# The last short cross-attention of a perceiver kernel rebuilt: raw contexts loaded in both layouts, context statistics taken in an earlier stage

## The reference

```python
def layernorm(x, g, b):
    mu = jnp.mean(x, axis=-1, keepdims=True)
    var = jnp.mean(jnp.square(x - mu), axis=-1, keepdims=True)
    return (x - mu) * jax.lax.rsqrt(var + EPS) * g + b
x1 = layernorm(modality1, ln1_g, ln1_b)
x2 = layernorm(modality2, ln2_g, ln2_b)
q = x1 @ Wq + bq
k = x2 @ Wk + bk
v = x2 @ Wv + bv
attn = jax.nn.softmax(jnp.einsum('bqe,bke->bqk', q, k) * scaling, axis=-1)
return jnp.einsum('bqk,bke->bqe', attn, v) @ Wo + bo
```

## Time and profile before

| what | us |
|---|---|
| median of 3 runs (lowest to highest) | 2023.21 (2018.51 to 2026.66) |
| profiled execution, its own time | 2018.47 |
| its span, first to last instruction | 2016.6 |
| TensorE busy over the span | 1633.3 (81%) |
| xattn2, first load issued to the last add | 930.7 to 1279.2 |
| xattn3, first instruction to the last add | 1556.2 to 1717.0 |
| TensorE busy, granted clock in 1556.2 to 1601 | 5.80 of 44.8, 0.50 |
| TensorE busy, granted clock in 1608 to 1717 | 93.81 of 109, 0.87 |

### The profile page before, as it was taken

How to read it: one execution, slowest core, us unless ns; L and a number is a source line. 1 busy time by engine, 2 the same in 40 slices (tenths; PEclk the granted TensorE clock), 3 DMA queues, 4 the chain that set the end, 5 groups by cost and what they waited for, 6 DMA issues and landing times. The chain is left out here.

```text
span 2016.6 us, 36051 instructions
## 1 busy us (share of the span) xinstructions
PE 1633.3 (81%) x12690; PEld 1402.0 (70%) x12690; DVE 1173.3 (58%) x3187; ACT 867.7 (43%) x2475; POOL 711.4 (35%) x780
## 2 busy tenths in 40 slices
PE   6999998650785999977999999699595388757996
PEld 6988997330465999946899889456494266546996
DVE  5666665688774888835666666289413565442222
ACT  4666664114543888812666666200131133112332
POOL 7655552541116999713000000177312211112111
PEclk9999999885896999987999999799697588858998
DMA  8444441010004333205222222520362210931112
GB/s 249 149 148 148 149 148 67 29 39 5 0 1 132 130 134 133 94 16 169 75 93 93 93 93 75 165 95 1 91 202 62 68 52 28 320 119 56 38 38 81
DMA packets 120795, 195.52 MB, mean 97 GB/s; under 512 B 17672, under 2 KB 87408, under 8 KB 120272
## 3 DMA queue, kind: packets, MB, share of 16 engines
q1 hardware_dynamic: 113504, 181.32, 27.3%
q0 software_dynamic: 3408, 8.54, 1.2%
q10 hardware_dynamic: 3712, 3.41, 0.6%
HBM read 154.16 MB, written 45.52 MB: 99 GB/s over the span
## 5 line engine op out<-in xcount | busy, mean ns | idle before, releaser
L672 DVE TENSOR_SCALAR xattn_oT<-bank,xattn_last 128x256 f32<-128x256 f32 x256 | 111.7, 478 | 100.1 <-PE bank L512 100.1
L592 ACT ACTIVATE xattn_probs<-bank,xattn_negmax 128x257 f32<-128x257 f32 x256 | 124.2, 485 | 57.8 <-DVE xattn_negmax L653 57.8
L653 DVE TENSOR_REDUCE xattn_negmax<-bank 128x1 f32<-128x257 f32 x256 | 108.0, 422 | 63.0 <-PE bank L485 61.3
L597 ACT ACTIVATE xattn_probs<-xattn_probs,xattn_rsum 128x257 f32<-128x257 f32 x256 | 131.9, 515 | 1.4 <-DVE xattn_rsum L657 1.4
L832 POOL TENSOR_SCALAR xattn_probs<-xattn_probs,xattn_rsum 128x257 f32<-128x257 f32 x128 | 119.9, 937 | 22.9 <-DVE xattn_rsum L1067 22.7
L1907 POOL MEMSET scan_decay<- 128x64 f32 x1 | 0.2, 214 | 337.1 <-POOLq L51 337.1
L603 ACT CAST xattn_probsT_hi<-bank 128x256 fp32r<-128x256 f32 x256 | 95.7, 374 | 40.4 <-PE bank L492 36.7
L662 DVE TENSOR_TENSOR xattn_probsT_lo<-bank,xattn_probsT_hi 128x256 fp32r<-128x256 f32 x256 | 104.9, 410 | 8.3 <-ACT xattn_probsT_hi L603 7.2
L492 PE MATMUL bank<-ident,xattn_probs 128*128 128x128 f32 x512 | 103.6, 285 | 2.5 <-ACT xattn_probs L597 2.0
L136 PE MATMUL bank<-ident,xn 128*128 128x128 f32 x144 | 32.6, 406 | 90.0 <-DVE xn L112 90.0
L481 PE MATMUL bank<-xattn_ctxT,xattn_qk_hi 128*128 128x258 f32 x256 | 93.6, 366 | 0.5 <-DVE xattn_qk L649 0.5
(11 more groups left out here) (500 smaller groups left out, 5426.1 us busy)
## 6 DMA issues: line engine op xcount, KB each, us to landing
xattn_ctxT<-ctx_partsT SPq DMA_DIRECT2D x64, 516.0 KB, 3.6
xattn_ctxN<-ctx_partsN SPq DMA_DIRECT2D x64, 384.0 KB, 3.1
ctx_partsT<-xattn_ctxT SPq DMA_DIRECT2D x32, 516.0 KB, 3.0
moe_w<-in_L_ffn_W SPq DMA_DIRECT2D x16, 1024.0 KB, 13.9
ctx_partsN<-xattn_ctxN SPq DMA_DIRECT2D x32, 384.0 KB, 3.9
moecap_w_early<-in_L_ffn_w SPq DMA_DIRECT2D x10, 1024.0 KB, 12.7
xattn_rawN<-in_ctx SPq DMA_DIRECT2D x32, 192.0 KB
moecap_w_late<-in_L_ffn_w SPq DMA_DIRECT2D x6, 1024.0 KB, 7.5
```

The lines of the kernel that those rows point to most:

```text
L592: nc.scalar.activation(probs[:, n % RING, :], SB[n % 2][:, 0:KV], ACT.Exp, bias=negmax[:, n % RING:n % RING + 1], accum_out=psum[:, n % RI ...
L597: nc.scalar.mul(probs[:, n % RING, :], probs[:, n % RING, :], rsum[:, n % RING:n % RING + 1]).then_inc(norm_ready, 1)
L653: nc.vector.tensor_reduce(negmax[:, n % RING:n % RING + 1], SB[n % 2][:, 0:KV], AX.X, ALU.max, negate=True).then_inc(negmax_ready, 1)
L672: nc.vector.tensor_scalar(oT[k][:, heads, b, :], by_head(OB[:, k * 2 * P:(k + 1) * 2 * P]), last[:, k, j * PER_TILE + b:j * PER_TILE + b + ...
```

## The change

1. The statistics of the context rows are taken in xattn2 (`cn` is given to that stage alone). SP loads the raw rows of every batch there too (same two shapes), DVE takes mean and variance in every step (one `bn_stats`, or three `bn_aggr` in each fourth step), and after the last unit POOL forms (variance + eps) to the powers 0.5 and -0.5 for all 96 groups of rows, PE transposes mean and both powers, ACT copies them out and SP stores them in DRAM (`ctx_rows`). A row-major copy stays in SBUF (`ctx_stat`).
2. xattn3 loads the context raw and in both layouts (`ctxT`, already an input, for the scores; the rows for the product). The mean is an extra row of the feature-major form and an extra column of the rows; the deviation is a second extra row and column. The scores are multiplied by 1/deviation of the key (DVE, `scaled`), the transposed probabilities by 1/deviation as they are copied, and the mean is subtracted when the result is normalised (`shift`). Statistics, normalisation, transposes of the context and their copies are gone from the stage.
3. Queries and queries to context are made for 512 tokens at once; values and projection for two tiles at once. All tiles are unrolled, with double buffers, three of the context, and each engine walks steps with fixed offsets. Loads stand on three semaphores, by when they are needed.
4. The double layer norm of x is done in one pass with one factor.

The first five pieces are of xattn2 (SP twice, POOL, PE, DVE at the end of step t = 4n + c), the last two of xattn3 (SP, PE). The first four `load_rows` of xattn2 stand behind all weights of the stage.

```diff
+def load_rows(n):
+    b = n % PER_TILE
+    if n >= PER_TILE:
+        sp.wait_ge(stats_done, (n - PER_TILE + 1) * KCH)
+    sp.dma_start(raw[:, b, 0:KCH - 1, :],
+                 d["ctx_768"][n, 0:(KCH - 1) * KP, :].rearrange("(c p) f -> p c f", p=KP)).then_inc(raw_loaded[b], 16)
+    sp.dma_start(raw[0:cn.LAST, b, KCH - 1, :], d["ctx_768"][n, (KCH - 1) * KP:KV, :]).then_inc(raw_loaded[b], 16)
...
+for n in range(PER_TILE):
+    load_rows(n)
...
+pool.wait_ge(mv_ready, cn.BLOCKS)
+nc.gpsimd.tensor_copy(cn.stat[:, 0, :], mv[:, :, 0]).then_inc(stat_ready, 1)
+nc.gpsimd.tensor_scalar(veps[:, :], mv[:, :, 1], EPS, None, ALU.add).then_inc(veps_ready, 1)
...
+for k in range(2):
+    nc.gpsimd.tensor_tensor(cn.stat[:, 1 + k, :], veps[:, :], half[:, k, :], ALU.pow).then_inc(stat_ready, 1)
...
+if cn and t == ALL + PV:
+    pe.wait_ge(stat_ready, 3)
+    for k in range(3):
+        mm = nc.tensor.transpose(SB[0][0:cn.BLOCKS, k * P:k * P + KP], cn.stat[:, k, :], core.ident[0:KP, 0:KP])
+    mm.then_inc(stat_turned, 1)
...
+def statistics(n, c):
+    dve.wait_ge(raw_loaded[n % PER_TILE], (n // PER_TILE + 1) * 32)
+    nc.vector.bn_stats(stats[:, n % 2, c, :], raw[:, n % PER_TILE, c, :]).then_inc(stats_done, 1)
...
+def load_keys(t):
+    z, of, sem = t % RING, tile_rows(d["ctxT"], t), T_loaded[t % RING]
+    if t >= RING:
+        sp.wait_ge(scores_done, t - RING + 1)
+    sp.dma_start(T1[:, z], of[:, 0:C1, :].rearrange("b p k -> p b k")).then_inc(sem, 16)
+    sp.dma_start(T2[0:C2, z], of[:, C1:CTX, :].rearrange("b p k -> p b k")).then_inc(sem, 16)
+    sp.dma_start(T2[C2:K2, z], cn.rows[0:2, t * PER_TILE:(t + 1) * PER_TILE, 0:KV]).then_inc(sem, 16)
+
+def load_rows(t):
+    z, of, sem = t % RING, tile_rows(d["ctx_768"], t), N_loaded[t % RING]
+    if t >= RING:
+        sp.wait_ge(pv_done, t - RING + 1)
+    for b in range(PER_TILE):
+        sp.dma_start(N[:, z, b, 0:KCH - 1, 0:CTX], of[b, 0:(KCH - 1) * KP, :].rearrange("(c p) f -> p c f", p=KP)).then_inc(sem, 16)
+    sp.dma_start(N[0:LAST, z, :, KCH - 1, 0:CTX], of[:, (KCH - 1) * KP:KV, :].rearrange("b p f -> p b f")).then_inc(sem, 16)
...
+def probs_ctx(t):
+    z = t % RING
+    pe.wait_ge(probsT_ready, 2 * (t + 1))
+    pe.wait_ge(N_loaded[z], (t // RING + 1) * 80)
```

More of the change, by code:

```diff
@@ L92, in dve @@
     def dve(self, dve, meanwhile=None):
[L94 to L113, removed]
@@ L115, in pool @@
-    def pool(self, pool, meanwhile=None):
-        nc = self.core.nc
[L118 to L129, removed]
+        nc, x, xn = self.core.nc, self.core.x, self.xn
@@ L704, in _ @@
                     add(j - 1)
+                if cn and t < ALL:
+                    n, c = divmod(t, GROUPS)
+                    if c < KCH:
+                        statistics(n, c)
+                    else:
+                        moments(n)
 def stage_clipped_attention(core, name, wq, wk, wv, wo, bo, bq, bk, bv, clamp):
@@ L3016, in _ @@
+            for t in range(RING):
+                moments(t)
+            pool.wait_ge(o_loaded, 80)
             pool.wait_ge(ln.xn_ready, TILES)
@@ new lines, in _ @@
+            extra_columns()
+            ln.pe(pe, 0)
+            queries(0)
+            ln.pe(pe, 1)
+            to_context(0)
+            for s in range(TILES + 5):
+                if s < TILES:
+                    if s < 2:
+                        pe.wait_ge(xT_ready, 2 * CD)
+                    scores(s)
+                if s == 0:
+                    queries(1)
+                if s == 1:
+                    to_context(1)
+                if 0 <= s - 1 < TILES:
+                    turn_probs(s - 1)
+                if 0 <= s - 3 < TILES:
+                    turn_out(s - 3)
+                if s >= 5 and s % 2:
+                    values((s - 5) // 2)
+                if s >= 6 and s % 2 == 0:
+                    project((s - 6) // 2)
+                if 0 <= s - 2 < TILES:
+                    probs_ctx(s - 2)
@@ new lines, in _ @@
+            to_context(0)
+            for s in range(TILES + 5):
+                if s == 0:
+                    act.wait_ge(o_loaded, 80)
+                if s < TILES:
+                    exp(s)
+                if s == 1:
+                    to_context(1)
+                if 0 <= s - 3 < TILES:
+                    turned_out(s - 3)
+                if s >= 5 and s % 2:
+                    values((s - 5) // 2)
+                if 0 <= s - 2 < TILES:
+                    normalise(s - 2)
@@ new lines, in _ @@
+            nc.vector.memset(sg2[C2:K2, :], 1.0).then_inc(ones_ready, 1)
+            ln.dve(dve)
+            extra_columns()
+            queries(0)
+            dve.wait_ge(rstd_loaded, 64)
+            for s in range(TILES + 5):
+                if s < TILES:
+                    largest(s)
+                if s == 0:
+                    queries(1)
+                if 0 <= s - 1 < TILES:
+                    probs_turned(s - 1)
+                if s >= 6 and s % 2 == 0:
+                    if s == 6:
+                        dve.wait_ge(bo_added, TILES)
+                    add((s - 6) // 2)
+                if 0 <= s - 2 < TILES:
+                    sums(s - 2)
```

588 lines of the change are left out of this document (282 added, 306 removed).

## The result

| | before | after |
|---|---|---|
| median (lowest to highest), same chip | 2023.22 us (2018.51 to 2026.66), 4 runs | 2076.69 us (2075.06 to 2079.66), 4 runs |
| profiled execution, its span | 2018.47, 2016.6 | 2075.06, 2073.2 |
| mean granted clock over the span | 0.894 | 0.876 |
| xattn2, from its own first layer-norm statistics to those of the next stage | 349.4 | 383.4 |
| the stages between | 277.7 | 278.5 |

The change makes the kernel slower: ratio 1.0268, 95% interval 1.0243 to 1.0292, which is 53.5 us between the medians. The forecast was 2063 us, or +39.9. The three stretches add to 55.4 of the 56.6 us by which the spans differ: xattn2 loses 34.0, xattn3 20.6.

The account below looks back on a forecast made before the run. Prediction: xattn3 is bound by row loads on few DMA engines, xattn2 by TensorE. Terms 6.6 + 7.3 + 2 + 24 = +39.9 us took the median from 2023.2 to 2063 us; range 2036 to 2082.

Parts of the forecast that it names:

- xattn3: Whole xattn3 stage: the row queue plus the work behind it ends at 167.4 instead of 160.8 us, +6.6 us.
- xattn2, start: Start of xattn2: first raw rows queue behind Wo, so the maximum of unit 1 comes late, +7.3 us.
- xattn2, units: Units of xattn2: DVE's added statistics and aggregates, 37 us of work into 97 free, cost +2 us.
- xattn2, end: End of xattn2: TensorE waits 21.1 us for two 15.1 us powers on POOL; with transposes and slow clock, +24 us.
- The bound of xattn3: xattn3: row loads of 86 and 85 partitions use few DMA engines and set the pace, 14.8 us a tile.
- rival 1: xattn3: rows no longer slow, TensorE bounds, stage takes 81 us instead of 160.8, kernel 1977 us; chance 0.11.
- the feature-major contexts: xattn3's SP queue: these new loads, 789 KB per tile, cost 2.4 us at 334 GB/s.
- The room above the forecast: Range up to 2082: 4 us for xattn2's end, 4 for its start, 11 for a third of the DVE bound.
- One of the signs: xattn3 timeline: DMA near 60 GB/s at a share near 0.2 while TensorE waits with its clock down.
- The tail's size: End of xattn3: product through final add behind the last rows, TensorE at the slow level, 15.1 us.
- Rival 2: End of xattn2: the power is cheap for many columns, so no wait; kernel 2040 us; chance 0.12.
- Rival 3: xattn2: DVE becomes the bound because statistics delay maxima TensorE waits for; 35 us more, 2098; chance 0.09.

Follow-up runs that it names:

- experiment 1: Changed kernel with xattn3's row loads cut at partition 80, one load taking a chunk of all four batches: 2013.68 us, ratio 0.9944.
- experiment 4: Kernel before the change with its own xattn3 row loads cut at partition 80, nothing else: 1991.92 us, ratio 0.9841.
- experiment 7: Changed kernel with each 86-partition row load of xattn3 cut into two of 43 partitions: 2172.59 us, one run.
- experiment 8: Changed kernel without the loads of xattn3's feature-major contexts from tile 3 on: 2055.32 us, ratio 1.0175.
- experiment 2: Changed kernel with POOL taking each batch's powers as soon as its moments are ready: 2052.73 us, ratio 1.0143.
- experiment 3: Changed kernel with xattn2's raw rows of the first two batches issued ahead of Wv and Wo: 2073.11 us, ratio 1.0230.
- experiment 6: Kernel before with its own xattn3 row loads cut at partition 80, timed again beside experiment 5: 1990.39 us, ratio 0.9861.
- experiment 5: Changed kernel with row loads of xattn3 and xattn2 cut at partition 80, powers per batch and first xattn2 rows early: 1971.82 us, ratio 0.9775.

## Why the prediction was right, and where it was off

| term | forecast | measured |
|---|---|---|
| xattn3 | +6.6 | +20.6 |
| xattn2, start | +7.3 | +4.9 |
| xattn2, units | +2 | +1.9 |
| xattn2, end | +24 | +27.1 |
| sum | +39.9 | +54.5 (spans: +56.6) |

The parts of xattn2 are measured from the stage's first statistics, at 930.76 and 930.68: to the maximum of unit 1, to the add at the end of the units, and to the next stage's statistics.

**The bound of xattn3 held.** Row loads in shapes of 86 and 85 partitions set its pace before and after; experiments 1, 4 and 7 show it from three sides, and rival 1 falls. That compute per tile would get shorter and gain nothing came true as well.

**The step that failed is a term of the sum: the feature-major contexts, "789 KB per tile, at the 334 GB/s of 128-partition loads 2.4 us".** They cost 4.3 us, 184 GB/s (experiment 8). By the pitch (19.0 in the five tiles shown, instead of 17.2) this is 14 us over eight tiles, and the last rows landed 13.3 us later than forecast, 165.6 us into the stage (from about 1591.4) and not 152.3. The rate had been read from other loads, the weights of the next stage. Experiment 1 shows what loads of this context get when the rows too come in 80 partitions and the engines are all busy: 213 GB/s, by which 789 KB take 3.7 of the 4.3 us (an estimate; rows and feature-major contexts are mixed in that stretch). So most of the error seems to be the rate of these loads themselves. What sets that rate, and the other 0.6 us behind rows that keep two engines busy, stays open. Narrow and wide loads do hinder each other in landing: from 1736 to 1739 the share is 1.00 at 230 GB/s, and from 1739 to 1740 it is down to 0.23, although scores start only at 1743.80. That the two busy engines are late with their part of the wide loads would explain this wait, but no run separates it from other causes.

**That the total lies within the range is partly luck.** The room above the forecast, up to 2082, was made for the end of xattn2, its start and DVE as its bound. The end of xattn2 took 3 us of it, the start came out below its forecast and DVE was no bound; what used up the rest, 14 us of xattn3, comes from a term that had no bound of its own. One of the signs was wrong in itself as well: 1579 KB in 17.2 us are 92 GB/s, not the "near 60" of the prediction, and measured are 86 at a share of 0.34.

**The tail's size was right by luck.** Forecast 15.1 us behind the last rows, measured 15.3 (1757 to 1772.3), of other parts. I had TensorE waiting for `xattn_N` at the slow level. In fact it waited for the feature-major contexts, which land late as well; the product of the last tile then came 4 us after its rows, because scores of the last tile and the steps behind them stand first in TensorE's order, and for that it ran at full clock (2.25 instead of 4.1). Experiment 8, where the rows do come last, has the slow level and 17 us (1736.30 to 1753.2), with the projection of another tile (3.62 us) in between, which the working had left out.

**The end of xattn2** went as worked out: 15.66 us for each power where the straight line through two sizes gave 15.1; TensorE idle 24.1 instead of 21.1. The clock behind the wait cost 4.6 us instead of 2, less about 2 us that the kernel before lost at this place too (20.7 us from the add to the next stage, 18.8 in experiment 2, which has more to do). Rival 2 falls. With the Trainium skill's rate for two-input operations (GPSIMD Engine Reference, section Elementwise), by my estimate well under 1 us for 96 columns, the trace does not agree where the operation is a power.

**The start** was 7.3 by the landing of Wo plus a batch's rows at the pace of xattn3; the rows landed 2.4 us sooner, at 959.2 instead of 961.6. Experiment 3 confirms the cause, in the trace more than in the time.

**The units** cost 1.9 us, but not by statistics that stand in the way, as the term had it: with the first rows in time they cost 0.1 (experiment 3). They fit the clock behind the wait at the start: TensorE stands 4.6 us until 960.96 and then works at the lower level, where the kernel before and experiment 3 have a granted clock of 1.00 in the same stretch:

```profile
960.00:965.00 5.00, 4.04 (x19) 4.04 (x20) 2.31 (x8) 3.13 (x11) 0.00 (x0) 0.50 0.17 53
```

Rival 3, DVE as the bound, falls too.

## What to carry to other kernels

A transfer that is slow at a low DMA share, as here, is short of engines and not of bandwidth: read share times 16 where nothing else moves, and look at the partition count of the load before rebuilding what hangs on it. Here cutting two loads of the old kernel gave 27 to 34 us (experiments 6 and 4), while the rebuilding, which kept the shape, lost 53; with the shape mended and two waits removed the same rebuilding gave 46. Price a load by a trace of its own kind or by leaving it out, not by the rate of other loads. Work moved "beside" another stage costs where its first input and its last output meet that stage's order, so feed it early and drain it piece by piece.

## What the runs showed of the hardware

- A power on POOL has a price by column: 0.862 us for 3 columns, 1.045 for 4, 2.27 for 12, 15.66 for 96, about 0.16 us a column. The copy of 96 columns beside it took 0.26 us.
- TensorE can be busy 84% of a stretch and be granted 0.50 (experiment 1), while xattn2 at 96% busy has 0.99. I had expected the slow level only where TensorE mostly waits. The same 24 products took 4.11 us there and 2.25 at full clock. This is one reason why rival 1's 81 us for the stage was not reached; another is that the first scores start 24.7 us behind the stage's first statistics (1619.84), where 13 were reckoned. What tells the two stretches apart stays open.
- With all 16 DMA engines busy, loads of the context went at 213 GB/s (share 1.13, experiments 1 and 5), the weights of the next stage at 334 (share 0.96).
- The same code of xattn3 took 114.3 us in experiment 1 and 108.6 in experiment 5, and 180.7 to 187.7 in three kernels with the changed kernel's form of it, so a single profile of this stage can be off by 6 or 7 us.
- Not tried: the product of the last tile but one ahead of the scores in TensorE's order, which might give back the 4 us at the end of the stage.
